# Transformer block, one core: q and k bias by matmul, scales on all partitions, ScalarE in the last tiles

## The chip, the cores and the metric

The kernel runs on one core of one Trainium2 chip. The metric is the device time of one execution in microseconds, the median over several runs; lower is better.

## The reference, cut to what matters

There are 2 sequences of 1024 tokens with 512 channels, 8 heads of 8 channels. Both halves of the block end in a layer norm without weights.

```
qk = x @ Wqk_w.T + Wqk_b            # q and k interleaved, 64 channels each
v  = x @ Wv_w.T + Wv_b
attn = softmax(q @ k.T, axis=-1) / sqrt(64)
x1 = layernorm(x + (attn @ v) @ Wo_w.T + Wo_b)
Wg, Wu, Wd = q[o, i] * s[o, i // 128]      # int4 values with one scale per 128 inputs
out = layernorm(x1 + (silu(x1 @ Wg.T) * (x1 @ Wu.T)) @ Wd.T)      # 1792 inner channels
```

## The kernel before, in words

The work is written out by hand as one instruction list per engine, tied together by counting semaphores; nothing plans it at run time. The batch index is b (2), a block of 512 tokens is u or blk (4), a tile is 128 tokens.

**The head.** SyncE loads the q,k weights, then x transposed in chunks of 128 channels x 512 tokens (`load_xt`, L417), with the bias column after the first four chunks (L419). TensorE runs ten f16 matmuls on a constant tile (L1078), then for b = 0 the projections of q and k for both blocks into PSUM banks 0 and 1 (`qk`, L892) and of v into bank 2 (`v`, L902). ScalarE adds the bias while it copies each bank to SBUF as f32 (`project_qk`, L716). VectorE takes the maximum of the absolute values of each row from this copy (`row_maxima`, L1196) and combines the two (L1202). TensorE turns the 128 maxima onto one partition (`turn_tops`, L925), VectorE reduces them to one number for q and one for k, makes powers of two and their reciprocals of them (`scale_row`, L1212 to L1221), a 1-row matmul spreads these over the partitions (`cast_scales`, L931) and three small copies put them in place as `unit` and `gamma` (`place_scales`, L1232, L1233). Then q and k are split in two f16 parts: ScalarE makes the high part, VectorE the low one (L733, L1241). TensorE places the parts in rows by selection matmuls (`put`, L946), and ScalarE copies each placed bank to SBUF (`keep`, L749, L752); the first maximum pass needs the first k rows and the first q rows. v is turned and copied into tiles that were cleared by VectorE before (L1187). The second batch goes the same way, in pieces between the maximum passes; its scales are worked on at steps 2 and 4 of the attention (`TOPS_AT`).

**Attention.** 256 maximum passes (`first_pass`, L963, reduced by VectorE at L1249) find the maximum of each row of scores ahead of its use. 46 of them stand before the first attention step, the others are spread over 64 steps of scores (L1039), exponentials on ScalarE (L760) and products with v (L1068). The passes share a ring of three PSUM banks in a fixed order (`ring_uses_at`), in which the turn and the spreading of the second batch's scales each take a place.

**Feed-forward.** 56 inner tiles (4 blocks x 14) run in periods: in each, 8 matmuls for the gate (L1123), 8 for up (L1135) and 8 for the down product of a tile three periods or more back (L1157). ScalarE and VectorE rescale in PSUM between groups. GpSimd splits the product of each period in two f16 parts (`inner_parts`, L661, L663), for which the down product waits, and has other work at fixed periods: the additions of finished blocks (L654), their inverse deviations and applies (L552, L554, L617), and ten products that scale the last block's residual (`scale_residual`, L674), one per period from 28 to 37.

**The end.** The last four tiles stay in PSUM. VectorE takes their statistics (L1428, L1473), GpSimd the inverse deviations of two tiles at a time (L552, L554), VectorE applies mean and inverse to all four (L1477), and SyncE stores each of them when it is ready (L510).

The ten periods of the residual products follow from one number, and the spreading of the scales has its place in the list of the first batch's pieces:

```
RESIDUAL_AT = 28
...
return [(qk, k, c) for k in range(2) for c in range(C)] + [(v, 0), (v, 1), (turn_tops, 0, bank[3]), (v, 2),
                                                           (cast_scales, 0, bank[3]), (v, 3), (vt,)]
```

Of the kernel before, what the change touches and what calls it, by code (L numbers as in the profile page):

```python
# [57 lines left out]
def build(nc, x, xT, wqkT, bqk, wvT, bv, woT, bo, gq, gs, uq, us, dq, ds, ds_next, spread, out):  # L58
    ctx = ExitStack()
    with ctx:  # L60
# [17 lines left out]
        onerow = sb("onerow", [1, P], F32)  # L78
        tops = sb("tops", [P, 3], F32)
        row = sb("row", [1, 8], F32)  # L80
# [40 lines left out]
        ident = sb("ident", [P, P], F32)  # L121

# [16 lines left out]
        rstd = sb("rstd", [P, BT], F32)  # L139

# [12 lines left out]
        s_bqk = sem("qk_bias_loaded")  # L153
        s_wv = sem("v_weights_loaded")
# [25 lines left out]
        s_cast = sem("scales_spread")  # L180
        s_unit = sem("scales_in_place")
# [4 lines left out]
        s_kept = sem("rows_kept_in_stack0")  # L186
        s_half = sem("second_half_q_rows_in_stack0")
# [39 lines left out]
        s_lastw = sem("last_tile_weights_and_row_scaled")  # L227
        s_res = sem("result_ready")
# [15 lines left out]
        TOPS_AT = {(2, 1): "tops", (4, 1): "cast"}  # L244
# [12 lines left out]
        def wait_ring_read(engine, kind, n):  # L257

            if kind == "first":
                engine.wait_ge(s_rr, n + 1)  # L260
            elif kind == "tops":
                engine.wait_ge(s_row, 6)
            elif kind == "cast":
                engine.wait_ge(s_unit, 6)
            else:
                engine.wait_ge(s_m0, 1)
# [78 lines left out]
        def put_bank(n):  # L345
            return bank[(0, 1, AVB)[n] if n < 3 else (AVB, 3)[(n - 3) % 2]]
# [168 lines left out]
        def _(pool):  # L515
# [6 lines left out]
            nc.gpsimd.memset(onerow[:], 1.0).then_inc(s_pick, 1)  # L522
            nc.gpsimd.memset(pick[:].bitcast(F32), 0.0).then_inc(s_pick, 1)
            pool.wait_ge(s_fill, 1)
            pool.wait_ge(s_pick, 2)
# [8 lines left out]
            pool.wait_ge(s_pick, 18)  # L534
# [36 lines left out]
            pool.wait_ge(s_fill, 6)  # L571
            def second_batch_parts():

                pool.wait_ge(s_unit, 6)
# [110 lines left out]
            for p in range(PERIODS):  # L685
                if 2 <= p < TILES + 1:
                    inner_parts(p - 2)
                if RESIDUAL_AT <= p < RESIDUAL_AT + len(residuals):
                    scale_residual(*residuals[p - RESIDUAL_AT])
# [7 lines left out]
                for blk in range(NB - 1):  # L697
# [5 lines left out]
                    if RESULT_AT[blk] + 2 <= p < RESULT_AT[blk] + 2 + BT:  # L703
                        pool.wait_ge(s_rstd, NB + blk + 1)
                        apply(blk, p - RESULT_AT[blk] - 2)
            inverse(2 * NB - 1, slice(0, 2), 2 * NB + 1)
            inverse(2 * NB, slice(2, 4), 2 * NB + 3)

        @block.scalar
        def _(act):  # L710
            def project_qk(b, k):

                act.wait_ge(s_proj, (1, 2, 4, 6)[2 * b + k])
                if b and k == 0:
                    act.wait_ge(s_low, 2)
# [12 lines left out]
            def high_parts():  # L728

                act.wait_ge(s_unit, 3)  # L730
                for k in range(2):
                    cols = slice(k * TB, (k + 1) * TB)
                    nc.scalar.activation(high[:, cols], qkf[:, cols], ACT.Copy, scale=unit[:, 0:1]).then_inc(s_high, 1)  # L733

            def place_v(b):

                act.wait_ge(s_vt, b + 1)
                if b == 0:
                    act.wait_ge(s_zero, 1)
# [14 lines left out]
            def exps(n, pair):  # L754

                pi, at = 2 * n + pair, shared_banks("scores", n, pair)
                act.wait_ge(s_scf, pi + 1)
                if n >= 2 and pair == 0:
# [58 lines left out]
            project_qk(1, 0)  # L817
# [6 lines left out]
            project_qk(1, 1)  # L824
# [38 lines left out]
            for p in range(PERIODS):  # L863
# [17 lines left out]
                slot(p, 3)  # L881

        @block.tensor
        def _(pe):
            def projections(b):


                def qk(k, c):
# [3 lines left out]
                    mm = nc.tensor.matmul(bank[k], wqk_s[:, c, :], xt[k][:, c, :], start=(c == 0), stop=(c == C - 1))  # L892
# [3 lines left out]
                def v(c):  # L896
                    if b and c == 0:
                        pe.wait_ge(s_projr, 3)
# [8 lines left out]
                def vt():  # L907
                    pe.wait_ge(s_projr, (3, 5)[b])
                    if b == 0:
                        pe.wait_ge(s_unit, 3)  # L910
# [4 lines left out]
                if b:  # L915
# [3 lines left out]
                                                                           (cast_scales, 0, bank[3]), (v, 3), (vt,)]  # L919

            def turn_tops(b, dst):
# [3 lines left out]
                nc.tensor.transpose(dst[0:1, 0:P], tops[:, 2:3], ident[:]).then_inc(s_rf if b else s_turned, 1)  # L925

            def cast_scales(b, dst):
                pe.wait_ge(s_row, 5 * (b + 1))
                if b == 0:
                    pe.wait_ge(s_pick, 1)  # L930
                nc.tensor.matmul(dst[:, P:P + 3], onerow[:], row[0:1, 4:7], start=True, stop=True)\  # L931
                  .then_inc(s_rf if b else s_cast, 1)

            def put(n):

                kind, k, t = placed[n]
                if n == 0:
                    pe.wait_ge(s_pick, 18)
# [4 lines left out]
                elif n >= 3:  # L943
                    pe.wait_ge(s_kept, max(n - 1, 3))
# [5 lines left out]
            def first_pass(n):  # L950
# [4 lines left out]
                if b == 0 and k == 0 and qt == 0 and jj == 0:  # L955
                    pe.wait_ge(s_kept, 3 * t + 2 + half)
# [14 lines left out]
            def ring_use(kind, n):  # L971
# [8 lines left out]
                elif kind == "cast":  # L980
                    cast_scales(n, ring_bank(kind, n))
# [38 lines left out]
            def scores(n, pair):  # L1020
# [10 lines left out]
                elif pi == 0:  # L1031

                    pe.wait_ge(s_vc, 2 * B)
                    pe.wait_ge(s_kept, len(placed))
                else:
                    pe.wait_ge(s_projr, 6)
# [147 lines left out]
        def _(dve):  # L1184
            nc.vector.memset(still[:].bitcast(F32), 1.0).then_inc(s_still, 1)
            nc.vector.memset(mhalf[:], -0.5).then_inc(s_const, 1)
            nc.vector.memset(arena[:, 2:4, :], 0.0).then_inc(s_zero, 1)  # L1187
            dve.wait_ge(s_zero, 1)
            for b in range(B):

                nc.vector.memset(vst[b][:, :, :, E:E + 1], float(HD) ** 0.5)

            def row_maxima(b, k):

                dve.wait_ge(s_projr, (1, 2, 4, 6)[2 * b + k])
                nc.vector.tensor_reduce(tops[:, k:k + 1], qkf[:, k * TB:(k + 1) * TB], AX.X, ALU.max,  # L1196
                                        apply_absolute_value=True).then_inc(s_top, 1)
# [6 lines left out]
            def scale_row(b):  # L1204
# [6 lines left out]
                src = at[0:1, 0:P].rearrange("p (a n) -> p a n", a=2)  # L1211
# [11 lines left out]
            def place_scales(b):  # L1223

                if b:
                    dve.wait_ge(s_rf, ring_count("cast", 1))
                else:
                    dve.wait_ge(s_cast, 1)
                at = ring_bank("cast", 1) if b else bank[3]
                for kind in range(2):  # L1230
                    own = slice(kind * HD, (kind + 1) * HD)
                    nc.vector.tensor_copy(unit[own, b:b + 1], at[own, P + kind:P + kind + 1]).then_inc(s_unit, 1)  # L1232
                nc.vector.tensor_copy(gamma[:, b:b + 1], at[:, P + 2:P + 3]).then_inc(s_unit, 1)  # L1233

            def low_parts():

                dve.wait_ge(s_unit, 3)
                for k in range(2):
                    cols = slice(k * TB, (k + 1) * TB)
                    dve.wait_ge(s_high, k + 1)  # L1240
                    nc.vector.scalar_tensor_tensor(out=low[:, cols], in0=qkf[:, cols], scalar=unit[:, 0:1],  # L1241
                                                   in1=high[:, cols], op0=ALU.mult, op1=ALU.subtract).then_inc(s_low, 1)

# [113 lines left out]
            for n in range(ALL):  # L1357
# [3 lines left out]
                for pair in range(2):  # L1361
                    for kind, m in ring_uses_at(n, pair):
                        if kind == "first":
                            first(m)
                        elif kind == "tops":
                            scale_row(1)
                        else:
                            place_scales(1)
# [105 lines left out]
            for i, k in enumerate(LAST_ORDER):  # L1474
# [47 lines left out]
```

## Time and profile before

| | |
|---|---|
| median of 3 runs | 521.45 us (521.42 to 521.49) |
| profiled execution, time | 521.81 us |
| profiled execution, span | 519.7 us |
| TensorE busy | 501.1 us, 96% |
| VectorE busy | 413.0 us, 79% |
| ScalarE busy | 405.5 us, 78% |
| GpSimd busy | 255.7 us, 49% |
| DMA | 29.20 MB, mean 56 GB/s |
| granted TensorE clock, mean | 0.998 |

The span runs from the first to the last instruction of the profiled execution; its time also has what lies around the span. Busy shares are means over stages: the head lasts until about 21 us, the attention until about 218 us, the feed-forward stage until about 511 us, and the last tiles follow. Matmul ends are modelled, so that a matmul's length includes its way through the array, and the spacing of starts tells its rate.

### The profile page before, as it was taken

The page shows a single profiled execution, that of the slowest core. Times are in us where ns is not written, and L with a number is a line of the kernel's source. Part 1 is how long each engine was busy: PE and PEld are TensorE (multiplying, and loading weights), DVE is VectorE, ACT ScalarE, POOL GpSimd, SP SyncE. Part 2 cuts the span into 40 slices and gives each one's busy share as a digit, 9 for nine tenths or more (in the row PEclk, how much of TensorE's full clock was granted, in tenths as well). Part 3 has the DMA queues.
Part 4 walks back from the last instruction along what each step waited for, and adds up shares of the span by engine and source line. Part 5 has one row for each costly group of instructions (what it writes and reads, how often), then busy time and mean ns, then how long its engine had stood idle before and what let it go on. Part 6 is the DMA issues. An engine that isn't in the chain of part 4 may idle for free.

```text
span 519.7 us, 8086 instructions
## 1 busy us (share of the span) xinstructions
PE 501.1 (96%) x2976; PEld 193.2 (37%) x2976; DVE 413.0 (79%) x705; ACT 405.5 (78%) x558; POOL 255.7 (49%) x295
## 2 busy tenths in 40 slices
PE   8899999999999999999999999999999999999994
PEld 3222222323222322234444444444444444444441
DVE  3699999989999997368878778778668666788677
ACT  1522888998899989877888888888888888888880
POOL 9100091823100715073464676664997962648741
PEclk9999999999999999999999999999999999999999
DMA  6410018576530005700031121140020020000022
GB/s 192 136 68 5 21 35 211 182 144 125 91 59 1 3 5 103 276 7 1 1 59 24 20 43 21 20 62 1 1 81 1 0 83 0 3 0 1 0 81 81
DMA packets 30151, 29.20 MB, mean 56 GB/s; under 512 B 19489, under 2 KB 21921, under 8 KB 29857
## 3 DMA queue, kind: packets, MB, share of 16 engines
q1 hardware_dynamic: 26688, 22.67, 15.7%
q0 software_dynamic: 3424, 6.03, 6.3%
q8 instruction: 23, 0.38, 0.3%
q14 instruction: 16, 0.12, 0.1%
HBM read 24.37 MB, written 4.23 MB: 55 GB/s over the span
## 4 chain that ended last, share of the span: by engine, by line
PE 79%; DVE 7%; POOL 5%; ACT 5%; issue 2%; DMA 1%; SPq 0%; DVEq 0%; POOLq 0%; ACTq 0%
PE ps L1123 16%; PE ps L1135 16%; PE ps L1157 16%; PE ps L1068 9%; PE ps L1039 6%; PE ps L963 6%; DVE mxh L1249 4%; ACT pbuf L760 3%; PE ps L892 3%; POOL x L617 2%; PE ps L1051 1%; PE ps L902 1%; PE ps L1016 1%; POOL stack L663 1%; DMA arena<-xT 1%
## 5 line engine op out<-in xcount | busy, mean ns | idle before, releaser
L1249 DVE TENSOR_REDUCE mxh<-ps 128x1 f32<-128x512 f32 x256 | 157.0, 680 | 6.5 <-PE ps L963 5.3
L760 ACT ACTIVATE pbuf<-ps,gamma 128x1024 f32<-128x1024 f32 x128 | 140.5, 1114 | 16.2 <-PE ps L1039 11.2
L841 ACT ACTIVATE ps<-ps,ratio 128x512 f32<-128x512 f32 x168 | 106.5, 659 | 40.4 <-PE ps L1123 37.3
L1157 PE MATMUL ps<-wd,stack 128*128 128x512 f16 x440 | 129.7, 379 | 0.7 <-POOL stack L663 0.6
L1123 PE MATMUL ps<-arena,wg 128*128 128x512 f16 x448 | 115.5, 379 | 0.1
L1135 PE MATMUL ps<-arena,wu 128*128 128x512 f16 x448 | 115.3, 379 | 0.1
L1423 DVE TENSOR_TENSOR ps<-ps,stack 128x512 f32<-128x512 f32 x128 | 87.8, 695 | 33.4 <-PE ps L1157 31.7
L847 ACT ACTIVATE ps<-ps,ratio 128x512 f32<-128x512 f32 x156 | 98.9, 659 | 6.6 <-PE ps L1135 2.3
L661 POOL CAST stack<-pbuf 128x512 f16<-128x512 f32 x55 | 33.5, 609 | 76.5 <-DVE pbuf L1398 76.5
L1423 DVE TENSOR_TENSOR ps<-ps,pbuf 128x512 f32<-128x512 f32 x76 | 52.6, 695 | 23.2 <-PE ps L1157 22.5
L1068 PE MATMUL ps<-pbuf,arena 128*32 128x256 f32 x832 | 66.5, 391 | 1.7 <-ACT avt L767 1.7
L663 POOL TENSOR_TENSOR stack<-pbuf,stack 128x512 f16<-128x512 f32 x55 | 63.7, 1157 | 4.5
L1123 PEld LDWEIGHTS ps<-arena,wg 128*128 128x128 f16 x448 | 43.2, 98 | 54.9 <-ACT pbuf L855 1.7
L1135 PEld LDWEIGHTS ps<-arena,wu 128*128 128x128 f16 x448 | 43.7, 98 | 53.3 <-DVE pbuf L1398 2.0
L1157 PEld LDWEIGHTS ps<-wd,stack 128*128 128x128 f16 x440 | 42.8, 98 | 53.2 <-issue 1.8
L963 PE MATMUL ps<-stack 64*128 64x512 f16 x256 | 60.8, 381 | 1.4 <-DVE mxh L1249 0.7
L563 POOL CAST mp<-mx 128x16 f16<-128x16 f32 x8 | 1.6, 196 | 108.1 <-DVE mx L1259 108.1
L1039 PE MATMUL ps<-stack 64*128 64x512 f16 x256 | 49.6, 386 | 1.9 <-ACT pbuf L760 1.6
L1398 DVE SCALAR_TENSOR_TENSOR pbuf<-ps,scales,pbuf 128x512 f32<-128x512 f32 x56 | 41.9, 748 | 6.4 <-PE ps L1135 6.1
L855 ACT ACTIVATE pbuf<-ps,scales 128x512 f32<-128x512 f32 x56 | 38.1, 680 | 0.2 <-PE ps L1123 0.2
L1039 PEld LDWEIGHTS ps<-stack 64*128 64x128 f16 x256 | 12.3, 92 | 58.2 <-issue 37.5
L963 PEld LDWEIGHTS ps<-stack 64*128 64x128 f16 x256 | 20.9, 94 | 34.2 <-DVE mxh L1249 31.2
(120 smaller groups left out, 387.4 us busy)
## 6 DMA issues: line engine op xcount, KB each, us to landing
arena<-xT SPq DMA_DIRECT2D x16, 256.0 KB, 5.8
x<-x SPq DMA_DIRECT2D x2, 2048.0 KB, 10.0
out<-x SPq DMA_DIRECT2D x3, 1024.0 KB, 4.2
stack<-down_ratios SPq DMA_DIRECT2D x1, 2048.0 KB, 9.6
wg<-gq POOLq DMA_DIRECT2D x4, 448.0 KB, 7.3
wu<-uq POOLq DMA_DIRECT2D x4, 448.0 KB, 7.4
wd<-dq POOLq DMA_DIRECT2D x2, 896.0 KB, 10.3
pbuf<-down_ratios SPq DMA_DIRECT2D x1, 1536.0 KB, 6.2
```

The source lines that it names most:

```text
L663: nc.gpsimd.tensor_tensor(mparts[:, 1, t % NM, :], sg[t % 2], mparts[:, 0, t % NM, :], ALU.subtract)\
L760: nc.scalar.activation(pbuf[:, pi % 4, :].rearrange("p (a n) -> p a n", a=2), ps[:, at:at + 2, :], ACT.Exp, scale=gamma[:, n // (ALL // B) ...
L841: nc.scalar.activation(gbank[t % 2], gbank[t % 2], ACT.Copy, scale=gr[:, t % G, c:c + 1])\
L847: nc.scalar.activation(ubank[t % 2], ubank[t % 2], ACT.Copy, scale=ur[:, t % G, c:c + 1])\
L963: nc.tensor.matmul(ring_bank("first", n), qs[b][rows, k, t, qt * P:(qt + 1) * P], ks[b][rows, t, half * TB:(half + 1) * TB], start=True, s ...
L1039: mm = nc.tensor.matmul(bank[at + j], ks[b][rows, t, kt * P:(kt + 1) * P], qs[b][rows, k, t, :], start=True, stop=True)
L1068: mm = nc.tensor.matmul(bank[AVB][j * VC:(j + 1) * VC, lo:hi], vst[b][:, kt, g * HG + j, :], pbuf[:, (2 * n + j // 2) % 4, (j % 2) * TB + ...
L1123: mm = nc.tensor.matmul(gbank[t % 2], wg[:, c, i * P:(i + 1) * P], x1v[blk][:, a, c, :, :], start=(c == 0 and a == 0), stop=(a == 1), skip ...
L1135: mm = nc.tensor.matmul(ubank[t % 2], wu[:, c, i * P:(i + 1) * P], x1v[blk][:, a, c, :, :], start=(c == 0 and a == 0), stop=(a == 1), skip ...
L1157: mm = nc.tensor.matmul(bank[k], mparts[:, a, t % NM, k * P:(k + 1) * P], wd[:, i, :], start=(i == 0 and a == 0), stop=(a == 1), skip_grou ...
L1249: nc.vector.tensor_reduce(mxh[:, f % 2, qh, half:half + 1], ring_bank("first", n), AX.X, ALU.max)\
L1423: nc.vector.tensor_tensor(dst, bank[k], by, ALU.mult).then_inc(s_dr[k], 1)
```

## The change

It does four things.

1. The q,k bias of the first batch enters PSUM by a matmul of a bias row with a row of ones, ahead of the projections. The row is loaded by a DMA on ScalarE's queue; the column is loaded later, for the second batch, which keeps ScalarE's bias pass. Six constant matmuls stand ahead of it instead of ten. The first batch's maxima, high and low parts read the PSUM banks; the placements change their banks, and VectorE copies the first q rows.
2. The turn of the maxima is four matmuls whose stationary operand is the maxima repeated over 64 columns, so that each partition gets all maxima of its own kind first and of the other behind. The scales are computed on all partitions, and the 1-row matmul and the three copies go, for both batches.
3. VectorE clears the first batch's v tile between its two maxima, GpSimd the second's after the low parts. The residual products stand at other periods.
4. In the last block GpSimd computes -mean x inverse, and ScalarE applies tiles 0 to 2; VectorE applies tile 3.

```diff
-        TOPS_AT = {(2, 1): "tops", (4, 1): "cast"}
+        TOPS_AT = {(2, 1): "tops"}
...
-            return bank[(0, 1, AVB)[n] if n < 3 else (AVB, 3)[(n - 3) % 2]]
+            return bank[(0, AVB, 1)[n] if n < 3 else (AVB, 3)[(n - 3) % 2]]
...
+        BY_ACT = 3
-        RESIDUAL_AT = 28
+        RESIDUAL_AT = (26, 27, 33, 34, 35, 40, 41, 42, 43, 44)
...  SyncE
-                    if b == 0 and k == 0:
-                        sp.dma_start(bqk_s[:], bqk).then_inc(s_bqk, 16)
             load_xt(0)
             sp.dma_start(wv_s[:], wvT).then_inc(s_wv, 16)
+            sp.dma_start(bqk_s[:], bqk).then_inc(s_bqk, 16)
...
-                sp.wait_ge(s_res, BT * (NB - 1) + i + 1)
+                if i < BY_ACT:
+                    sp.wait_ge(s_resa, i + 1)
+                else:
+                    sp.wait_ge(s_res, BT * (NB - 1) + i - BY_ACT + 1)
                 sp.dma_start(out[t], x1[:, t, :]).then_inc(s_out, 16)
...  GpSimd
+            pool.wait_ge(s_low, 2)
+            nc.gpsimd.memset(arena[:, 3, :], 0.0).then_inc(s_zero1, 1)
+            pool.wait_ge(s_zero1, 1)
+            nc.gpsimd.memset(vst[1][:, :, :, E:E + 1], float(HD) ** 0.5).then_inc(s_zero1, 1)
...
+            def last_shift(n, tiles):
+                nc.gpsimd.tensor_scalar(negm[:, tiles], mv[:, tiles, 0], -1.0, None, ALU.mult).then_inc(s_neg, 1)
+                pool.wait_ge(s_neg, n + 1)
+                pool.wait_ge(s_rstd, 2 * NB + n)
+                nc.gpsimd.tensor_tensor(shift[:, tiles], negm[:, tiles], rstd[:, tiles], ALU.mult).then_inc(s_shift, 1)
             inverse(2 * NB - 1, slice(0, 2), 2 * NB + 1)
+            last_shift(0, slice(0, 2))
             inverse(2 * NB, slice(2, 4), 2 * NB + 3)
+            last_shift(1, slice(2, 3))
...  ScalarE
-                act.wait_ge(s_unit, 3)
+                act.wait_ge(s_row, 4)
...
-                    nc.scalar.activation(high[:, cols], qkf[:, cols], ACT.Copy, scale=unit[:, 0:1]).then_inc(s_high, 1)
+                    nc.scalar.activation(high[:, cols], bank[k], ACT.Copy, scale=unit[:, 0:1]).then_inc(s_high, 1)
...
+            act.dma_start(brow[:], bqk.rearrange("p o -> o p")).then_inc(s_brow, 16)
...
-            act.wait_ge(s_bqk, 16)
-            for k in range(2):
-                project_qk(0, k)
             high_parts()
             act.wait_ge(s_fill, 3)
-            for n in range(3):
-                keep(n)
+            keep(0)
+            keep(2)
             project_v(0)
...
+            for i, k in enumerate(LAST_ORDER[:BY_ACT]):
+                act.wait_ge(s_bn, BT * (2 * NB - 1) + i + 1)
+                act.wait_ge(s_shift, i // 2 + 1)
+                nc.scalar.activation(x1[:, (NB - 1) * BT + k, :], bank[k], ACT.Identity, bias=shift[:, k:k + 1],
+                                     scale=rstd[:, k:k + 1]).then_inc(s_resa, 1)
...  TensorE
-                return [(qk, k, c) for k in range(2) for c in range(C)] + [(v, 0), (v, 1), (turn_tops, 0, bank[3]), (v, 2),
-                                                                           (cast_scales, 0, bank[3]), (v, 3), (vt,)]
+                                                                           (v, 3), (vt,)]
...
-                nc.tensor.transpose(dst[0:1, 0:P], tops[:, 2:3], ident[:]).then_inc(s_rf if b else s_turned, 1)
+                for own in range(2):
+                    for kind in range(2):
+                        at = HD * (kind != own)
+                        mm = nc.tensor.matmul(dst[own * HD:(own + 1) * HD, at:at + HD], tops[:, 2:3].to_broadcast([P, HD]),
+                                              ident[:, kind * HD:(kind + 1) * HD], start=True, stop=True)
+                mm.then_inc(s_rf if b else s_turned, 1)
...
-            for _ in range(10):
+            for _ in range(6):
                 nc.tensor.matmul(bank[7], still[:, 0:P], still[:], start=True, stop=True)
+            pe.wait_ge(s_brow, 16)
+            pe.wait_ge(s_ones, 1)
+            for k in range(2):
+                nc.tensor.matmul(bank[k], brow[:], ones[:], start=True, stop=False, skip_group_check=True)
...  VectorE
-                src = at[0:1, 0:P].rearrange("p (a n) -> p a n", a=2)
+                src = at[:, 0:P].rearrange("p (a n) -> p a n", a=2)
...
-                nc.vector.reciprocal(row[:, 4:6], row[:, 2:4]).then_inc(s_row, 1)
-                nc.vector.tensor_tensor(row[:, 6:7], row[:, 2:3], row[:, 3:4], ALU.mult).then_inc(s_row, 1)
+                nc.vector.reciprocal(unit[:, b:b + 1], row[:, 2:3]).then_inc(s_row, 1)
+                nc.vector.tensor_tensor(gamma[:, b:b + 1], row[:, 2:3], row[:, 3:4], ALU.mult).then_inc(s_row, 1)
...
+            def keep_first_q():
+                dve.wait_ge(s_put, 2)
+                nc.vector.tensor_copy(qs[0][:, 0, 0, :], put_bank(1)).then_inc(s_kept1, 1)
...
-            for k in range(2):
-                row_maxima(0, k)
+            row_maxima(0, 0)
+            clear_first_v()
+            row_maxima(0, 1)
             combine_tops(0)
             scale_row(0)
-            place_scales(0)
             low_parts()
+            keep_first_q()
...
-            for i, k in enumerate(LAST_ORDER):
+            for i, k in list(enumerate(LAST_ORDER))[BY_ACT:]:
```

## Rows read from the trace of the kernel before

**Rows 1.** Windows: length, then busy us (instructions) per engine, granted clock, DMA share, GB/s.

```profile
60.00:66.00 6.00, 5.79 (x52) 1.78 (x51) 5.80 (x17) 4.74 (x5) 0.83 (x4) 1.00 0.00 0
420.00:500.00 80.00, 80.00 (x372) 36.29 (x371) 58.36 (x90) 67.67 (x108) 44.81 (x44) 1.00 0.07 27
516.00:518.00 2.00, 0.00 (x0) 0.00 (x0) 1.25 (x2) 0.00 (x0) 0.00 (x0) 0.94 0.95 365
```

**Rows 2.** Timeline of TensorE's start: start, length, work, count, idle before and its releaser.

```profile
1.18 4.45 PE L1078 MATMUL ps<-still 128*128 128x512 f16 x10 [1.18 <-DVE still L1185]
5.78 1.10 PE L892 MATMUL ps<-arena,wqk_s 128*128 128x512 f32 x2 [0.15 <-DMA arena<-xT]
7.24 6.28 PE L892 MATMUL ps<-arena,wqk_s 128*128 128x512 f32 x14 [0.36 <-DMA arena<-xT]
```

**Rows 3.** DMA issues: count, KB each, us from issue to landing.

```profile
wqk_s<-wqkT SPq DMA_DIRECT2D x1, 256.0 KB, 2.8
bqk_s<-bqk SPq DMA_DIRECT2D x1, 0.5 KB, 5.7
```

**Rows 4.** Timeline from the second maximum to the first maximum pass.

```profile
14.27 0.69 DVE L1196 TENSOR_REDUCE tops<-x 128x1 f32<-128x512 f32 x1 [2.68 <-ACT x L716]
15.62 0.28 DVE L1212 TENSOR_REDUCE row<-ps 1x2 f32<-1x128 f32 x1 [0.47 <-PE ps L925]
16.32 0.15 DVE L1220 RECIPROCAL row<-row 1x2 f32<-1x2 f32 x1
17.56 1.33 ACT L733 ACTIVATE x<-x,unit 128x512 f16<-128x512 f32 x2 [3.32 <-DVE gamma L1233]
19.30 1.46 PE L946 MATMUL ps<-x,pick 128*128 128x512 f16 x6 [1.33 <-DVE x L1241]
21.22 0.39 PE L963 MATMUL ps<-stack 64*128 64x512 f16 x2 [0.46 <-ACT stack L752]
```

**Rows 5.** Chain of waits, in order of time: start, length, engine, line.

```profile
15.38 0.20 PE ps L925
16.59 0.38 PE ps L931 x2
```

**Rows 6.** Timeline near 65 us: the second batch's scales.

```profile
64.36 0.38 PE L931 MATMUL ps<-row,onerow 1*128 1x3 f32 x2 [0.21 <-DVE mxh L1249]
65.63 0.33 DVE L1232 COPY unit<-ps 64x1 f32<-64x1 f32 x2
```

**Rows 7.** Timeline of TensorE near 384 and 390 us.

```profile
383.84 1.03 PE L1123 MATMUL ps<-arena,wg 128*128 128x512 f16 x4
385.43 0.59 PE L1157 MATMUL ps<-wd,stack 128*128 128x512 f16 x2 [0.56 <-POOL stack L663]
...
389.74 1.03 PE L1123 MATMUL ps<-arena,wg 128*128 128x512 f16 x4
390.89 0.59 PE L1157 MATMUL ps<-wd,stack 128*128 128x512 f16 x2
```

**Rows 8.** Timeline of GpSimd ahead of it.

```profile
360.96 1.27 POOL L674 TENSOR_TENSOR x<-x,wqk_s 128x512 f32<-128x512 f32 x1
...
363.65 2.09 POOL L617 TENSOR_SCALAR x<-x,mv,rstd 128x512 f32<-128x512 f32 x1
...
381.00 2.49 POOL L654 TENSOR_TENSOR x<-wob,x 128x512 f32<-128x512 f32 x2
...
384.13 1.15 POOL L663 TENSOR_TENSOR stack<-pbuf,stack 128x512 f16<-128x512 f32 x1
```

**Rows 9.** Timeline of the last tiles.

```profile
512.89 0.24 POOL L552 TENSOR_SCALAR veps<-mv 128x2 f32<-128x2 f32 x1 [6.48 <-DVE mv L1473]
513.21 0.73 POOL L554 TENSOR_TENSOR rstd<-veps,mhalf 128x2 f32<-128x2 f32 x1
...
514.31 2.93 DVE L1477 TENSOR_SCALAR x<-ps,mv,rstd 128x512 f32<-128x512 f32 x4
515.12 2.49 SPq L510 DMA_DIRECT2D out<-x  x4
```

More of the change, by code:

```diff
@@ L77, in build @@
         kbias = sb("kbias", [P, 1], F32)
-        onerow = sb("onerow", [1, P], F32)
         tops = sb("tops", [P, 3], F32)
-        row = sb("row", [1, 8], F32)
+        row = sb("row", [P, 4], F32)
         unit = sb("unit", [P, B], F32)
@@ L121, in build @@
         ident = sb("ident", [P, P], F32)
+        brow = sb("brow", [1, P], F32)
+        ones = sb("ones", [1, TB], F32)
         mhalf = sb("mhalf", [P, BT], F32)
@@ L139, in build @@
         rstd = sb("rstd", [P, BT], F32)
+        negm = sb("negm", [P, BT], F32)
+        shift = sb("shift", [P, BT], F32)
         ps = ctx.enter_context(nc.psum_tensor("ps", [P, 8, TB], F32))
@@ L153, in build @@
         s_bqk = sem("qk_bias_loaded")
+        s_brow = sem("qk_bias_row_loaded")
+        s_ones = sem("ones_row_set")
+        s_zero1 = sem("second_v_zeroed")
         s_wv = sem("v_weights_loaded")
@@ L227, in build @@
         s_lastw = sem("last_tile_weights_and_row_scaled")
+        s_neg = sem("last_means_negated")
+        s_shift = sem("last_shifts_ready")
+        s_resa = sem("last_results_by_act")
         s_res = sem("result_ready")
@@ L262, in wait_ring_read @@
                 engine.wait_ge(s_row, 6)
-            elif kind == "cast":
-                engine.wait_ge(s_unit, 6)
             else:
@@ L757, in exps @@
                 act.wait_ge(s_scf, pi + 1)
+                if pi == 0:
+                    act.wait_ge(s_row, 5)
                 if n >= 2 and pair == 0:
@@ L891, in qk @@
                         pe.wait_ge(s_kept, k + 1)
-                    mm = nc.tensor.matmul(bank[k], wqk_s[:, c, :], xt[k][:, c, :], start=(c == 0), stop=(c == C - 1))
+                    mm = nc.tensor.matmul(bank[k], wqk_s[:, c, :], xt[k][:, c, :], start=(b == 1 and c == 0), stop=(c == C - 1),
+                                          skip_group_check=True)
                     if c == C - 1:
@@ L942, in put @@
                     pe.wait_ge(s_vc, 2)
-                elif n >= 3:
-                    pe.wait_ge(s_kept, max(n - 1, 3))
+                elif n == 3:
+                    pe.wait_ge(s_kept1, 1)
+                elif n > 4:
+                    pe.wait_ge(s_kept, n - 2)
                 for part in range(2):
@@ L955, in first_pass @@
                 if b == 0 and k == 0 and qt == 0 and jj == 0:
-                    pe.wait_ge(s_kept, 3 * t + 2 + half)
+                    pe.wait_ge(s_kept, 3 * t + 1 + half)
+                    pe.wait_ge(s_kept1, 1)
                 elif n == H * BT * 2:
@@ L1186, in _, with clear_first_v @@
             nc.vector.memset(mhalf[:], -0.5).then_inc(s_const, 1)
[L1187 to L1191, printed above, removed]
-            def row_maxima(b, k):
-                dve.wait_ge(s_projr, (1, 2, 4, 6)[2 * b + k])
-                nc.vector.tensor_reduce(tops[:, k:k + 1], qkf[:, k * TB:(k + 1) * TB], AX.X, ALU.max,
-                                        apply_absolute_value=True).then_inc(s_top, 1)
+            nc.vector.memset(ones[:], 1.0).then_inc(s_ones, 1)
+            def clear_first_v():
+                nc.vector.memset(arena[:, 2, :], 0.0).then_inc(s_zero, 1)
+                dve.wait_ge(s_zero, 1)
+                nc.vector.memset(vst[0][:, :, :, E:E + 1], float(HD) ** 0.5)
+            def row_maxima(b, k):
+                if b:
+                    dve.wait_ge(s_projr, (2, 4)[k])
+                    src = qkf[:, k * TB:(k + 1) * TB]
+                else:
+                    dve.wait_ge(s_proj, k + 1)
+                    src = bank[k]
+                nc.vector.tensor_reduce(tops[:, k:k + 1], src, AX.X, ALU.max, apply_absolute_value=True).then_inc(s_top, 1)
             def combine_tops(b):
@@ L1219, in scale_row @@
                 dve.wait_ge(s_row, 5 * b + 3)
-                nc.vector.reciprocal(row[:, 4:6], row[:, 2:4]).then_inc(s_row, 1)
-                nc.vector.tensor_tensor(row[:, 6:7], row[:, 2:3], row[:, 3:4], ALU.mult).then_inc(s_row, 1)
[L1223 to L1233, printed above, removed]
+                nc.vector.reciprocal(unit[:, b:b + 1], row[:, 2:3]).then_inc(s_row, 1)
+                nc.vector.tensor_tensor(gamma[:, b:b + 1], row[:, 2:3], row[:, 3:4], ALU.mult).then_inc(s_row, 1)
             def low_parts():
-                dve.wait_ge(s_unit, 3)
+                dve.wait_ge(s_row, 4)
                 for k in range(2):
@@ L1240, in low_parts @@
                     dve.wait_ge(s_high, k + 1)
-                    nc.vector.scalar_tensor_tensor(out=low[:, cols], in0=qkf[:, cols], scalar=unit[:, 0:1],
+                    nc.vector.scalar_tensor_tensor(out=low[:, cols], in0=bank[k], scalar=unit[:, 0:1],
                                                    in1=high[:, cols], op0=ALU.mult, op1=ALU.subtract).then_inc(s_low, 1)
+            def keep_first_q():
+                dve.wait_ge(s_put, 2)
+                nc.vector.tensor_copy(qs[0][:, 0, 0, :], put_bank(1)).then_inc(s_kept1, 1)
             def reduce(n):
@@ L1364, in _ @@
                             first(m)
-                        elif kind == "tops":
+                        else:
                             scale_row(1)
-                        else:
-                            place_scales(1)
                     for kind, f, _ in turns_at(n, pair):
```

50 lines of the change are left out of this document (20 added, 30 removed).

## The prediction

> **What bounds the kernel now.** I read the windows first, because shares over the whole span mix stages. Their columns are busy time per engine; the reader is to see that in the feed-forward stage TensorE is busy for all of 80 us, that in the attention stage it shares the bound with VectorE (5.79 and 5.80 of 6 us), and that in the last microseconds no engine but the DMA is full, 0.95 at 365 GB/s [rows 1]. So an edit pays where it shortens the serial head ahead of the first maximum pass, where it takes VectorE work out of the attention stage, where it takes a hole out of TensorE's row in the feed-forward stage, or where it lets the last store leave earlier. The timeline of the first 22 us comes next (start, length, in brackets the idle time and who ended it), then the landings of the DMAs, the chain of waits between 15 and 17 us, and TensorE and GpSimd side by side around 384 us.
>
> **Step 1, the bias by matmul, up to the end of the projections.** Before, ten f16 matmuls of 512 columns run from 1.18 us, 4.45 us together, that is 0.43 us each: 512 columns at 1.2 GHz. The record calls the granted clock 1.00 there, so the level has to be read from the spacing. At 19.30 six of the same size take 1.46 us, 0.24 each, the 2.4 GHz level. A projection matmul in f32 is two instructions; the first two take 1.10 us at 5.78, fourteen take 6.28 us, 0.45 each, so the level had risen by 5.8 us, after 4.6 us of full matmuls [rows 2, 4]. Now six f16 matmuls end at 1.18 + 6 x 0.43 = 3.8 us, and two f32 matmuls of one row follow, four instructions at 0.86 each while the clock is low: two until about 5.5, the others at 0.43 to 6.4. Nothing was waiting for them: the first projection pair takes 0.86, ends at 7.3, and the second chunk of x landed at 7.24, where TensorE had idled 0.36 us [rows 2]. Cost 0.1 us. From below it is 0; a gain is excluded, since the x chunks set the pace. From above it is four instructions at 0.86 that start only when the row has landed. That landing is not in the trace: the weights ahead of it took 2.8 us to land, the bias column behind 1.25 MB on SyncE's queue took 5.7 [rows 3]. The row goes alone on ScalarE's queue at about 0.7 us, 512 B in a single partition, so I take the 2.8, a landing at 3.5, ahead of need.
>
> The Trainium skill (DMA: Bandwidth & Descriptors, Anatomy of one DMA) gives a DMA about 2.0 us of fixed cost, fitted on GpSimd's path; by that the row would be there at about 2.7 us and the sum would be the same. No run so far shows a DMA of that queue.
>
> **Step 2, maxima from PSUM, scales on all partitions.** Before, ScalarE adds the bias to the second half before VectorE's maximum at 14.27 can start, which costs 0.7 us. That goes, so the combined maximum is ready at about 14.5 instead of 15.15. But next late is TensorE, which is in order and busy with the v matmuls until 15.38 [rows 5]; the turn can start at about 15.2 instead of 15.31, so of 0.7 us only 0.1 is won. The turn itself was one instruction of 0.27 us and becomes four f32 matmuls, eight instructions of 64 columns with a weight load each. The nearest row is the pair of 1-row matmuls, 0.38 for two, which is 0.25 for the last one and 0.13 of spacing [rows 5]. At 0.10 to 0.13 of spacing eight end 0.7 x 1.2 + 0.22 = about 1.0 us after the start, at 16.15. Bounds: 0.6 (paced by 64 columns only) and 1.5 (0.19 each). VectorE's row reduction then starts at 16.15 instead of 15.62, and the reciprocal ends 0.85 later (16.32 + 0.15 - 15.62), at 17.0 [rows 4]. Gone are the 1-row matmul and three copies: ScalarE's high parts start at 17.03 instead of 17.56. Gain 0.53, from 0.05 to 0.9 over the bounds.
>
> **Step 3, the first q rows kept by VectorE.** From the high parts to the first maximum pass it is 3.66 us before (17.56 to 21.22), the end of which is ScalarE's two evictions in turn. Now ScalarE does the first, and VectorE the q rows, which are ready after four of the six matmuls (19.30 + 0.97 + 0.2 = 20.5) and take about 0.69 like the reduction of that size [rows 4]: 21.15 on the old clock, 0.05 to 0.15 better. ScalarE is also 0.6 us less busy and the later placements wait less for it, perhaps 0.1 more. With step 2 this makes **0.8 us** (0.2 to 1.2) by which the maximum passes start and run earlier. VectorE's 3.5 us clearing at the start is split: half stands between the two maxima (10.9 to 12.7 or at worst 13.2 us, the second maximum needs 13.5), half on GpSimd, idle after 14.6. Both are hidden; if the first were not, it would delay by its overrun.
>
> **Step 4, second batch's scales.** In the stage shared by VectorE and TensorE [rows 1] a matmul pair of 0.38 with 0.21 of waiting, and three copies (0.33 for two, half of that for the third, 0.5 in all) disappear near 65 us [rows 6]. Against that the turn at 58.8 grows by about 0.7 us of TensorE, of which TensorE's waits for VectorE take most. Half of what VectorE loses passes through: **0.3 us** gained, bounds 0.7 gained and 0.3 lost.
>
> **Step 5, residual products moved.** In the feed-forward stage a group of four matmuls lasts 0.86 us. The group at 383.84 should be followed at 384.70 and is at 385.43: 0.73 us lost, and the idle time is put down to GpSimd's split. The one at 389.74 is followed at 390.89 instead of 390.60, 0.29 more [rows 7]. A period is 24 matmuls of 0.216, 5.18 us. In it GpSimd runs a split of 1.8 and, from period 28 to 37, a residual product of 1.25; an apply of 2.09 comes on top in periods 28 to 31, an inverse of 1.4 in 28 (362.23 to 363.65), two additions of 2.49 in 31 and 32 [rows 8]. The loads of 28 to 31 are 6.6, 5.1, 5.1 and 7.6, so by the surplus over 5.18 GpSimd is 3.7 us behind at the split of period 32, and its end at 385.28 makes TensorE 0.73 late: some 3.0 us of lateness cost nothing. With the products moved to 26, 27, 33 to 35 and 40 to 44, no period with an apply or additions carries one: the loads of 28 to 33 are 5.3, 3.9, 3.9, 6.4, 4.3 and 3.1, and it is at most 1.3 us behind. The products are needed from period 45 on, and the last is done in 44. The two holes close: **1.0 us**, from 0 (another cause ends last there) to 1.02, all that these rows hold.
>
> **Step 6, the last four tiles.** Before, VectorE applies them in 2.93 us from 514.31, 0.73 each, and the stores are issued from 515.12, the last near 517.27 (2.49 less an issue of 0.34) [rows 9]. Now GpSimd first has two more small operations per pair, each about 0.24 plus 0.08 of gap like the one at 512.89. The first inverse ends at 513.94, the shifts at 514.57, ScalarE (0.67 per tile, from two in 1.33) ends tiles 0 and 1 at 515.27 and 515.94. GpSimd's second pair starts 0.16 late and ends at 516.33, ScalarE ends tile 2 at 517.03. VectorE has tile 3 long before (516.4), but SyncE is in order and stores it last: issues at 517.05 and 517.4. The two stores now come together, 256 KB each at 365 GB/s being 0.72 us [rows 1]: the last data ends 517.05 + 2 x 0.72 instead of 517.27 + 0.72. That is **0.5 us slower**; bounds 0 (small operations of 0.1) and 0.8. A table load for the biased pass, if one is needed, is hidden in ScalarE's idle time from 507 on.
>
> **Sum.** +0.1 - 0.8 - 0.3 - 1.0 + 0.5 = -1.5 us. The profiled execution took 521.81, 2.1 outside its span of 519.7; the median of the runs is 521.45. 1.5 less is 520.3 for a profiled one and **519.9** for the median. Everything between 66 us and the end hangs on waits between engines, so a shift of the head passes on.
>
> **Rivals.**
> A (0.62): the forecast, own range 519.0 to 520.8.
> B, the clock (0.14): the six matmuls plus one-row ones don't raise TensorE to 2.4 GHz by 5.8 us, or the row lands as late as the column did and TensorE idles from 3.8. For it: only 2.6 us of full matmuls are left where 4.45 were, and a row of 5.7 us. Against: four more instructions fill the time. Price: with the row at 0.7 + 5.7 = 6.4 us and four instructions at 0.86, the projections start at 9.8 instead of 5.8 and run on unbroken for 6.9, to 16.7 instead of 13.5: 3.2 more than the forecast, 523.1. With the row on time and only the clock low, each f32 instruction costs 0.43; it decides from the fourth (break-even), and the seventh makes it slower than measurement can hide.
> The Trainium skill (TensorE: Matmul & The Clock Gate, Part 1: The HAM clock gate) says that the throttled level is the default and sustained activity releases it; its section on PE-mode transpose says that not every kind of work counts alike. It warns against this change; the trace agrees that the first ten ran low.
> C, the turn (0.12): eight small instructions each as slow as an isolated one (0.25) take 2 us. For: a weight load for each. Against: the pair of 0.38. Step 2 then gives -0.5 lost instead of 0.53 gained, step 4 gains nothing: -0.2 in all, 521.2.
> D, a hidden hole (0.12): GpSimd's time was not what ended last at 384 us, or the hole reopens elsewhere. For: the row names one releaser only. Against: GpSimd is idle-free from 359. Step 5 gives 0: -0.5, 520.9.
>
> **How the numbers follow.** About 0.2% (1.0 us) is what a measurement here can tell from no change. Faster by more: 0.58 from A, 0.02 from B, 0.04 from C, 0.03 from D, 0.67. Slower by more: 0.08 from B, 0.01 each from C and D, 0.10. The rest, 0.23. The range takes in A with its bounds, D and C: 518.6 to 521.4.
>
> **What would show it.** Six matmuls, then four instructions to 6.4 us, projections ending at 13.5 (B: later, at 0.86 each). Eight turn instructions in 1.0 us, high parts at 17.0, first maximum pass at 20.4. No idle piece of TensorE between 350 and 400 us. Last two stores 0.4 us apart at the end. Wrong if the projections end after 14 us or the feed-forward stage keeps its 1.0.

## The result and the profile after

The changed kernel takes 523.88 us (median of 4 runs, 522.91 to 524.64) beside 521.43 us before (521.18 to 521.49): a ratio of 1.0047, 95% interval 1.0029 to 1.0064. The forecast was 519.9. The profiled execution took 523.83 us with a span of 521.7, 2.0 longer than before. Two executions that ran far longer (1697.71 us of the kernel before, 710.75 us of one experiment) are left out of the ranges below.

The timeline of TensorE in the first 24 us (start, length, work, count):

```profile
1.18 2.74 PE L1105 MATMUL ps<-still 128*128 128x512 f16 x6 [1.18 <-DVE still L1216]
3.85 3.78 PE L1109 MATMUL ps<-ones,brow 1*128 1x512 f32 x4
7.56 9.27 PE L918 MATMUL ps<-arena,wqk_s 128*128 128x512 f32 x16
16.76 1.94 PE L929 MATMUL ps<-arena,wv_s 128*64 128x512 f32 x8
18.52 0.45 PE L955 MATMUL ps<-ident,tops 128*64 128x64 f32 x8
23.53 0.39 PE L991 MATMUL ps<-stack 64*128 64x512 f16 x2 [0.44 <-DVE stack L1272]
```

The row was there in time: the bias matmuls follow the constant ones with no releaser named. But the four instructions take 3.78 us, and sixteen projection instructions 9.27, where fourteen took 6.28 [rows 2]. The weight loads between them show why (PEld: weight loads; bracket: idle before):

```profile
10.29 0.34 PEld L918 LDWEIGHTS ps<-arena,wqk_s 128*128 128x128 f32 x1 [0.52 <-issue]
11.14 0.34 PEld L918 LDWEIGHTS ps<-arena,wqk_s 128*128 128x128 f32 x1 [0.52 <-issue]
11.95 0.19 PEld L918 LDWEIGHTS ps<-arena,wqk_s 128*128 128x128 f32 x1 [0.47 <-issue]
12.38 0.19 PEld L918 LDWEIGHTS ps<-arena,wqk_s 128*128 128x128 f32 x1 [0.24 <-issue]
```

Until 11.9 us they come every 0.86 us, afterwards every 0.43: 1.2 and then 2.4 GHz. The windows call the granted clock 1.00 in this stretch too, so in them only the spacing shows it. The trace itself agrees with the spacing: its first entry of a granted clock, 1.00, stands at 11.89 us, and at 5.78 us in the trace of before, and the windows extend it back to the start. These entries give the moment of the rise for every run below. The projections therefore end 3.3 us late, and the first maximum pass stands at 23.53 instead of 21.22 [rows 4].

In the feed-forward stage both holes of [rows 7] are gone: no matmul of the down product waits for GpSimd any more. At the end the first store leaves at 516.18 instead of 515.12, 1.1 us later, though the last down products begin only 0.7 us later than before (510.11 instead of 509.38):

```profile
515.09 0.19 POOL L724 TENSOR_TENSOR shift<-negm,rstd 128x2 f32<-128x2 f32 x1
515.36 0.23 POOL L559 TENSOR_SCALAR veps<-mv 128x2 f32<-128x2 f32 x1
515.37 1.45 ACT L906 ACTIVATE x<-ps,shift,rstd 128x512 f32<-128x512 f32 x2 [7.61 <-POOL shift L724]
516.18 2.51 SPq L518 DMA_DIRECT2D out<-x  x4
516.42 0.81 DVE L1506 TENSOR_SCALAR x<-ps,mv,rstd 128x512 f32<-128x512 f32 x1 [1.30 <-POOL rstd L561]
516.79 0.19 POOL L724 TENSOR_TENSOR shift<-negm,rstd 128x1 f32<-128x1 f32 x1
517.08 0.78 ACT L906 ACTIVATE x<-ps,shift,rstd 128x512 f32<-128x512 f32 x1 [0.26 <-POOL shift L724]
```

VectorE has the fourth tile at 517.2, but the third comes at 517.9 and goes first. The windows (length, busy per engine, granted clock, DMA share, GB/s) show stores still moving after 520:

```profile
516.00:518.00 2.00, 0.00 (x0) 0.00 (x0) 0.81 (x1) 1.60 (x3) 0.82 (x3) 0.77 0.48 184
518.00:520.00 2.00, 0.00 (x0) 0.00 (x0) 0.00 (x0) 0.00 (x0) 0.00 (x0) 0.50 0.83 316
520.00:521.00 1.00, 0.00 (x0) 0.00 (x0) 0.00 (x0) 0.00 (x0) 0.00 (x0) 0.50 0.15 55
```

Laid against the trace of before, the span's 2.0 us are: +2.3 to the first maximum pass, -0.6 from there to the first gate matmul (193.9 us instead of 194.5), -1.0 from there to the last down products, +1.3 from those to the end (11.6 instead of 10.3).

### The profile page after: what moved, and what is told of

Its sections match the earlier page's. It is cut to its first block, busy times and chain, and to the rows that moved or that the text cites. A ratio compares the mean times of both kernels' runs of the same rounds, so it can differ in the third digit from the quotient of the medians.

```text
span 521.7 us, 8112 instructions
## 1 busy us (share of the span) xinstructions
PE 504.0 (97%) x2986; PEld 195.1 (37%) x2986; DVE 409.5 (78%) x697; ACT 405.8 (78%) x558; POOL 258.6 (50%) x300
## 4 chain that ended last, share of the span: by engine, by line
PE 87%; DVE 5%; ACT 4%; issue 2%; POOL 1%; POOLq 0%; ACTq 0%; DVEq 0%
PE ps L1154 18%; PE ps L1166 18%; PE ps L1188 18%; PE ps L1095 9%; PE ps L991 6%; PE ps L1066 6%; PE ps L918 3%; ACT pbuf L783 3%; DVE mxh L1279 3%; PE ps L1078 1%; PE ps L1042 1%; PE ps L929 1%; PE ps L973 1%; ACT avt L790 1%; PE ps L1029 1%
```

## The experiments

"Less" and "more" are of medians. The runs were made in three groups, and the kernel before was run beside each: 521.72 in the first, 521.88 in the second, 521.75 in the third.

**More constant matmuls** (in the changed kernel)

```diff
-            for _ in range(6):
+            for _ in range(10):
```

> The changed kernel with ten constant matmuls instead of six ahead of the bias matmuls. Theory K (TensorE stays at its lower level because the one-row bias matmuls replace full ones): the level rises near 5.8 us as in the kernel before, the four bias instructions take 0.43 us each after the first, the projections start near 7.2 and end near 14.1 us instead of 16.8, and the kernel takes 2.7 us less than the changed one, about 521.2. Rival W (a one-row f32 matmul takes 0.86 us at any level, the clock has nothing to do with it): bias from 5.5 to 8.9 us, projections end near 15.8, about 522.9.

Twelve runs fell into two groups: seven from 520.5 to 521.7 and five from 525.2 to 525.4 us. The profiled one, 525.25 us, belongs to the second:

```profile
1.18 4.45 PE L1105 MATMUL ps<-still 128*128 128x512 f16 x10 [1.18 <-DVE still L1216]
5.56 3.78 PE L1109 MATMUL ps<-ones,brow 1*128 1x512 f32 x4
9.27 9.38 PE L918 MATMUL ps<-arena,wqk_s 128*128 128x512 f32 x16
```

After the same ten full matmuls as before (full: all 128 rows fed), the four one-row instructions ran low and so did the first projections behind them; the level rose at 13.82 us. The time of the first group is what theory K said, though none of its executions was profiled; the second fits neither theory: with one-row matmuls behind them, ten full matmuls are enough in some executions only.

**The bias matmul on all rows**

```diff
-        brow = sb("brow", [1, P], F32)
-        ones = sb("ones", [1, TB], F32)
+        brow = sb("brow", [P, P], F32)
+        ones = sb("ones", [P, TB], F32)
...
+            nc.vector.memset(brow[:], 0.0).then_inc(s_bz, 1)
...
+            act.wait_ge(s_bz, 1)
+            act.dma_start(brow[0:1, :], bqk.rearrange("p o -> o p")).then_inc(s_brow, 16)
```

> The changed kernel with the bias row standing in row 0 of a 128-row tile that is otherwise zero, and the ones on all 128 partitions: the same sum, the same number of instructions, but all rows of the array are fed. Theory K1 (what counts is that the matmuls use one row of the array): the level rises by about 6 us, the bias ends near 6.5 us, projections end near 13.6, the kernel takes 3.2 us less than the changed one, about 520.7. Rival K2 (what counts is the number of f16 matmuls, or f32 work counts less, or the zeros don't count as work): nothing changes, about 523.9.

520.61 us (519.82 to 521.29, eleven runs), ratio to before 0.9976 (0.9967 to 0.9985), 3.3 less than the changed kernel by the medians of two groups of runs, and no late group. The sum is the same and so are the instructions; only the other 127 rows are fed, with zeros:

```profile
3.71 3.46 PE L1111 MATMUL ps<-ones,brow 128*128 128x512 f32 x4
7.01 7.33 PE L920 MATMUL ps<-arena,wqk_s 128*128 128x512 f32 x16
21.06 0.39 PE L993 MATMUL ps<-stack 64*128 64x512 f16 x2 [0.45 <-DVE stack L1275]
```

This is the slowest of the eleven: the level rose at 6.88 us, and the projections end 2.5 us earlier than in the changed kernel's trace. In the two traces of the repaired kernel further down it rose at 4.76 and 5.12.

**One-row constant matmuls in the kernel before**

```diff
-                nc.tensor.matmul(bank[7], still[:, 0:P], still[:], start=True, stop=True)
+                nc.tensor.matmul(bank[7], still[0:1, 0:P], still[0:1, :], start=True, stop=True)
```

> The kernel before, whose ten constant f16 matmuls take one row of the array each (one partition of the constant tile) instead of 128; number, columns, type and times at the lower level are the same. Theory K1 (TensorE's level rises by work that feeds the rows of the array): it doesn't rise by 5.8 us, the projections (128 rows, f32) run at 0.86 us per instruction until they have raised it, 4 to 8 of them, so 1.3 to 3 us more than before, about 523.5, with a spread of a microsecond or more between executions. Rival K2 (f32, or the zeros of the other experiment, made the difference and rows don't count): 521.4 as before.

523.89 us (522.94 to 524.18, five runs), ratio 1.0038 (1.0026 to 1.0050): K1 again, from the other side and in f16. The level rose at 11.14 us.

```profile
1.18 4.44 PE L1078 MATMUL ps<-still 1*128 1x512 f16 x10 [1.18 <-DVE still L1185]
6.27 9.52 PE L892 MATMUL ps<-arena,wqk_s 128*128 128x512 f32 x16 [0.65 <-DMA arena<-xT]
```

**Six constant matmuls in the kernel before**

```diff
-            for _ in range(10):
+            for _ in range(6):
```

> The kernel before with six constant matmuls instead of ten, nothing else; TensorE idles from 3.8 us to the first projection at 5.8. Theory K in its wide form (six full matmuls are not enough, whatever follows): the level rises late, some four to six projection instructions take 0.86 instead of 0.43 us, of which 0.4 us is hidden by the DMA, 1.3 to 2.2 us more than before, about 523. Rival (six are enough, it is the one-row matmuls that keep the level low): 521.4.

522.96 us (521.96 to 524.4, eleven runs), ratio 1.0026 (1.0017 to 1.0035): the wide form of K holds for the median. The profiled execution is the fastest of them, 521.96. There the level rose at 4.55 us, while TensorE stood idle after 2.7 us of full matmuls, and the projections ran at 0.45 us from 5.72 on. By their times most of the other executions had it later.

**VectorE's tail in the changed kernel**

```diff
-        BY_ACT = 3
+        BY_ACT = 0
...
-            last_shift(0, slice(0, 2))
...
-            last_shift(1, slice(2, 3))
```

> The changed kernel with the last four tiles applied by VectorE as before (no shifts on GpSimd, no passes on ScalarE). The trace puts the end of the last tile's down product 0.7 us later than before and the end of the span 2.0 us later. Theory T (the new tail costs the difference, 1.3 us, through the later start of the first store and the bunching of the last two): 1.3 us less than the changed kernel, about 522.6. Rival (part of the 1.3 is a slow last transfer of this one execution, and the tail costs the 0.5 us of the forecast): about 523.4.

522.61 us, but in two groups again: four runs of 518.5 to 520.7 and eight of 522.5 to 523.6. The profiled one, 518.54 us, had the high level from 3.96 us, during the bias matmuls:

```profile
3.85 2.02 PE L1107 MATMUL ps<-ones,brow 1*128 1x512 f32 x4
5.80 7.13 PE L916 MATMUL ps<-arena,wqk_s 128*128 128x512 f32 x16
12.86 1.94 PE L927 MATMUL ps<-arena,wv_s 128*64 128x512 f32 x8
```

The last three of the four bias instructions start 0.43 us apart here, so rival W of the first experiment is out: a one-row f32 instruction takes 0.86 us at the lower level only. From the last down products to the end it takes 10.3 us, as before the change. The median agrees with theory T, but with such a spread it can't carry it; the next two do.

**The tail alone, on the kernel before** (its diff is that of the change, SyncE's, GpSimd's, ScalarE's and VectorE's lines of the last block)

> The kernel before with ScalarE applying three of the last tiles and GpSimd computing the shifts, nothing else. Theory T (the new tail alone costs 1.3 us, as the distance from the last tile's down product to the end of the span, 10.3 us before and 11.6 to 11.8 with it, has it): 1.3 us more, about 522.8. Rival (in the changed kernel the tail is slow because of what stands before it): 0.5 us or less.

522.26 us (521.83 to 523.15), ratio 1.0011 (1.0002 to 1.0020): 0.5 us more by the medians, 0.1 to 1.0 by the interval. In its trace the distance from the last down products to the end is 11.2 us, 0.8 more. So by time the rival's size is nearer here, by trace neither.

**The new periods alone**

```diff
-        RESIDUAL_AT = 28
+        RESIDUAL_AT = (26, 27, 33, 34, 35, 40, 41, 42, 43, 44)
```

> The kernel before with the residual products of the last block at the new periods, nothing else. Theory P (GpSimd's backlog made TensorE's two holes near 384 and 390 us, 1.0 us together): the holes are gone, 1.0 us less, about 520.4 beside 521.4. Rival (something else ends last there, or in the changed kernel it was the shift of the whole stage): no difference.

520.70 us (519.51 to 522.72), ratio 0.9981 (0.9970 to 0.9992), 1.2 less than before in the same group. Two of the twelve runs lie at 522.5 and 522.7; neither was profiled. In the profiled one the holes are closed, a group of four is followed after 0.86 us throughout:

```profile
380.85 1.03 PE L1123 MATMUL ps<-arena,wg 128*128 128x512 f16 x4
381.71 0.59 PE L1157 MATMUL ps<-wd,stack 128*128 128x512 f16 x2
```

**Scales on all partitions and new periods, bias on ScalarE** (the change's second point and the periods, on the kernel before)

```diff
-                nc.tensor.transpose(dst[0:1, 0:P], tops[:, 2:3], ident[:]).then_inc(s_rf if b else s_turned, 1)
+                for own in range(2):
+                    for kind in range(2):
+                        at = HD * (kind != own)
+                        mm = nc.tensor.matmul(dst[own * HD:(own + 1) * HD, at:at + HD], tops[:, 2:3].to_broadcast([P, HD]),
+                                              ident[:, kind * HD:(kind + 1) * HD], start=True, stop=True)
...
-            place_scales(0)
```

> The kernel before with the scales on all partitions (turn by four matmuls, no spreading matmul, no three copies, both batches) and the new periods; the bias stays on ScalarE, the constant matmuls are ten, the tail is VectorE's. Theory S: TensorE's eight turn instructions take 0.45 us, the high parts start about 0.9 us earlier than before, the second batch's scales give 0.6, the periods 1.0: 2.5 us less, about 518.9, and little spread. Rival (the head's gain needs the maxima from PSUM): 0.2 us instead of 0.9, about 519.7.

519.46 us (519.12 to 519.69), ratio 0.9954 (0.9942 to 0.9966): 1.2 less than the periods alone. The rival is out: the turn and the later steps gain without the maxima from PSUM.

```profile
13.55 1.94 PE L900 MATMUL ps<-arena,wv_s 128*64 128x512 f32 x8
15.32 0.45 PE L926 MATMUL ps<-ident,tops 128*64 128x64 f32 x8
20.42 0.39 PE L959 MATMUL ps<-stack 64*128 64x512 f16 x2 [0.46 <-ACT stack L748]
```

**Both repairs: bias on all rows, VectorE's tail**, run twice, in the second and the third group

> The changed kernel with the bias matmul on all 128 rows and the last tiles applied by VectorE. If the two effects found add up (3.3 us for the level, 1.3 us for the tail): 519.3. Rival (the tail costs the forecast 0.5 us): 520.1.

> The best version so far a second time, beside the changed kernel on the same chip: bias matmul on all rows, last tiles by VectorE. 2.5 us less than the kernel before, 4.6 less than the changed one.

519.13 us (518.69 to 519.75), ratio 0.9951 (0.9938 to 0.9964), and 519.16 (518.87 to 519.28), ratio 0.9952 (0.9940 to 0.9964). It beats both kernels. Against the one with only the first repair, the tail is worth 1.5 us by the medians and 1.3 by the ratios to before, of two groups of runs. The two traces are of the same kernel, and the level rose at 4.76 us in one and at 5.12 in the other. In the trace of the first:

```profile
3.72 2.40 PE L1109 MATMUL ps<-ones,brow 128*128 128x512 f32 x4
5.96 7.08 PE L918 MATMUL ps<-arena,wqk_s 128*128 128x512 f32 x16
12.96 1.94 PE L929 MATMUL ps<-arena,wv_s 128*64 128x512 f32 x8
19.75 0.39 PE L991 MATMUL ps<-stack 64*128 64x512 f16 x2 [0.44 <-DVE stack L1273]
```

**The changed kernel again**

> The changed kernel itself, to see how its executions are spread. Theory K1 (one-row matmuls don't raise TensorE's level, and the moment at which it rises differs from execution to execution): two groups, most near 523.9, some near 520.5 where the level happened to rise before the bias matmuls. Rival (the level rises at a fixed moment): one group within 0.5 us of 523.9.

Twelve runs, median 523.44, ratio 1.0019 (0.9998 to 1.0040): four from 519.9 to 520.1 and eight from 523.2 to 524.7. The profiled one, of the second group, has the sixteen projection instructions in 10.18 us instead of 9.27; the level rose at 13.72 us instead of 11.89, in the same kernel. So the moment at which the level rises isn't fixed. The early group lies 1.7 us below the kernel before, near the forecast 1.5, and the median of a series depends on how many of its executions are early.

## Why the prediction was wrong, by its own steps

**Step 1 failed.** It said that four instructions would run two at 0.86 us and two at 0.43, and cost 0.1 us, because the 4.6 us of matmuls ahead of the rise would be filled as before. The one-row instructions fill the time but don't raise the level. With the ten f16 constant matmuls on one row and nothing else changed, it stayed low until 11.14 us; with 128 rows fed, none of 21 runs fell into a late group. In the profiled execution the projections ended 3.3 us late, and this is the whole reversal: feeding all rows gives 3.3 us back by the medians. Part of it is chance: in 4 of 12 later executions the level rose in time all the same.

It was rival B, given 0.14, which took two causes together. The late row did not happen; the clock did. Its 3.2 us, priced for the late row, agree with the 3.3 by luck. Its price for the clock holds, 0.43 us per instruction, and so does "the seventh makes it slower than measurement can hide": by the rise near 11.9 us all four bias instructions, two more than forecast, and five projections had paid it, 7 x 0.43 = 3.0 of the 3.3 us. B's weight was too small because "four more instructions fill the time" took a busy engine for an array whose rows are all fed, and no row of the trace showed that: before, TensorE had nothing but 128-row work ahead of the rise.

One more sentence of step 1 failed, "a gain is excluded, since the x chunks set the pace". Where the level was high early, the projections ended at 12.86 to 13.10 us (the three traces of the changed head with an early rise) instead of 13.45: the second chunk of x landed at 5.7 to 6.6 us there, not at 7.2.

The prediction cited the Trainium skill (TensorE: Matmul & The Clock Gate, Part 1: The HAM clock gate) as a warning. By that rule, that the throttled level is the default and activity releases it, the trace agrees: in every run the first matmuls of 512 columns start 0.43 us apart. That the release also varies from run to run, which the same part states, was left out of the forecast and shows here: 11.89 and 13.72 us in two executions of the changed kernel.

**Step 2, mis-sized.** The turn was put at 1.0 us for eight instructions, with 0.6 as the lower bound; they take 0.45. From the v projections to ScalarE's high parts it is 3.2 us instead of 4.1 (12.96 to 16.15 in the repaired kernel beside 13.45 to 17.56), a gain of 0.9 where 0.53 stood; the maxima from PSUM give almost nothing of it, because TensorE is busy with v, as the step said: the kernel without them has 0.9 too (13.55 to 16.76).

**Step 3.** High parts to the first pass: 3.59 us instead of 3.66, at the lower end of 0.05 to 0.15. The further 0.1 that the step hoped for was not found: steps 2 and 3 together give 1.0 in the trace where 0.8 stood.

**Step 4, mis-sized but in its bounds:** 0.6 instead of 0.3 (the stretch from the first pass to the first gate matmul, 194.5 to 193.9 us, in the kernel with the scales and the periods alone as well). Most of the 0.7 us of removed work and waiting passed through, not half.

**Step 5 right:** 1.0 in the trace; alone it measured 1.2 with an interval of 0.4 to 1.6.

**Step 6, right in mechanism and size, with a term missing:** 0.5 was forecast; the trace of the changed kernel has 1.3 and the pair of repaired kernels 1.3 to 1.5, beyond the bound of 0.8, while on the kernel before it is 0.5 by time and 0.8 by trace. Each store is moved by the core's 16 DMA engines, and the trace records when each of them is done. Before, all 16 have finished the last store 9.9 us after the last down products begin. In all five traces with the new tail, 15 of the 16 have finished it after 10.5 us, 0.5 later: the forecast. In these 0.5 us are ScalarE's pass, 0.78 us and not 0.67, and the two stores that come together, whose parts land 0.67 us one after the other. But the sixteenth engine is 0.76 us later in the changed kernel's trace, and 0.25 to 0.94 in the other four. The share of one engine in 16 is 0.06; here it is seen working alone:

```profile
520.50:521.00 0.50, 0.00 (x0) 0.00 (x0) 0.00 (x0) 0.00 (x0) 0.00 (x0) 0.50 0.05 20
```

What the forecast did not know is a load of 8 KB of instructions (DMA queue 14), which runs amid the stores in these five traces, from 518.91 to 519.64 us in the changed kernel's. In the eight traces with VectorE's tail no such load falls among the stores, and the last store lands 2.0 to 2.2 us after its issue. That the load holds up the sixteenth engine is likely from this, but no run moved it alone, and why it falls there only with the new tail is open.

That the early group of the changed kernel lies near the forecast is in part luck. The only trace of such a head is that of the changed kernel with VectorE's tail, and against the kernel before it has -0.6 us to the end of the projections (forecast +0.1), -1.0 to the first pass (-0.8), -0.6 to the first gate matmul (-0.3) and -1.0 to the last down products (-1.0). With the 1.3 of the new tail (+0.5) that is an estimate of -1.9, where the group measured -1.7 and the forecast said -1.5.

## What to carry to other kernels

Warm-up work and what stands in for it should feed all rows of the array (only one row and 128 were tried here); replacing a full matmul by a one-row one of the same length can leave everything behind it at half rate until the level rises, even when TensorE looks busy. Read the level from the spacing of equal matmuls and profile more than one execution where the head is short, for the moment of the rise moves. Zeros in the unused rows were enough: with 127 rows of them in the bias matmuls, none of 21 runs was late. Before handing a last tile to a second engine, follow the in-order store queue: two results that arrive together are stored one after the other, and look in the trace's DMA queues for transfers that are not the kernel's own.

## What was not expected of the hardware

Eight f32 matmuls of 64 columns with a weight load each took 0.45 us; they start in pairs, 0.06 us from pair to pair, while two 1-row ones with 128 columns of weights took 0.38 [rows 5]. Ten f16 matmuls of 512 columns at the low level took 4.45 us whether 128 rows or one were fed, 4.45 and 4.44; only what followed differed. With six full matmuls ahead, the level rose at 4.55 us although TensorE had been idle since 3.9.
